# A three-stage transformer kernel on one Trainium2 core: first norm of the last stage made one stage earlier, turned context stored and reloaded, block rounding rewritten, order of the steps in the two last stages changed

## The reference

```python
x = x + tanh(g_xattn[0]) * mha16(layernorm(x), ctx)            # 16 heads of 32, with biases
x = x + tanh(g_ffn[0])   * ffn0(layernorm(x))                  # ternary weights, 8 bit activations, SiLU gate, 2048 wide
x = x + tanh(g_xattn[1]) * (softmax(layernorm(x) @ ctx.T) @ ctx)
x = x + tanh(g_ffn[1])   * (fp4(layernorm(x)) @ fp4(w1).T + bias)

def fp4(x):                                                    # blocks of 32 numbers
    amax  = max(abs(x), per block)
    scale = 2 ** (floor(log2(amax)) - 2) * 2 ** (0.5 * tanh(4 * delta))
    a     = clip(abs(x / scale), 0, 6)
    step  = 2 ** (clip(floor(log2(a)), 0, 2) - 1)
    return scale * sign(x) * round(a / step) * step
```

## Time and profile before

| | us |
|---|---|
| median of the runs | 1857.91 |
| profiled execution, its own time | 1863.25 |
| its span, first to last instruction | 1861.5 |
| last score starts to end of the span | 31.4 |

### The profile page before, as it was taken

The page is one execution under the profiler, slowest core; times in us unless marked ns, Lnnn a source line. Parts: engine busy times, 40 slices in busy tenths (PEclk is TensorE's granted clock), DMA queues, the critical chain, the costliest instruction groups (busy, mean ns, idle before and its releaser), DMA issues. The chain is left out here.

```text
span 1861.5 us, 27434 instructions
## 1 busy us (share of the span) xinstructions
PE 1575.9 (85%) x7400; PEld 1010.4 (54%) x7433; DVE 1330.4 (71%) x2277; ACT 868.4 (47%) x1433; POOL 898.3 (48%) x1098
## 2 busy tenths in 40 slices
PE   5889898989988899997257999999997588878886
PEld 3656555655655556652254544544443476666664
DVE  3676666757676667764755888888885488989886
ACT  3354545545554546544474545555453334444431
POOL 3265665656665666666002323223230366666653
PEclk9899998999999998997588999999998799999998
DMA  5627272543637272620802444444442212111110
GB/s 181 182 81 208 64 205 62 152 130 114 164 102 187 63 206 73 168 71 12 323 24 75 111 108 101 105 106 108 104 99 65 80 52 68 69 63 68 64 51 34
DMA packets 192668, 200.15 MB, mean 108 GB/s; under 512 B 94508, under 2 KB 111416, under 8 KB 192056
## 3 DMA queue, kind: packets, MB, share of 16 engines
q1 hardware_dynamic: 192568, 199.06, 38.4%
HBM read 119.05 MB, written 58.72 MB: 96 GB/s over the span
## 5 line engine op out<-in xcount | busy, mean ns | idle before, releaser
L488 ACT ACTIVATE a_probs<-a_sc 128x512 f32<-128x512 f32 x512 | 301.1, 596 | 330.5 <-PE a_sc L402 282.1
L543 DVE TENSOR_REDUCE a_negmax<-a_mx 128x1 f32<-128x512 f32 x512 | 337.5, 676 | 109.3 <-PE a_mx L385 107.3
L597 POOL TENSOR_TENSOR a_acc<-a_acc,a_probs 128x512 f32<-128x512 f32 x256 | 319.8, 1281 | 6.9 <-ACT a_probs L488 5.5
L597 POOL TENSOR_TENSOR a_acc<-a_probs 128x512 f32<-128x512 f32 x128 | 162.0, 1284 | 222.7 <-ACT a_probs L488 221.8
L385 PE MATMUL a_mx<-a_stack 96*128 96x512 f32 x512 | 230.2, 450 | 31.3 <-DVE a_negmax L543 19.5
L402 PE MATMUL a_sc<-a_stack 97*128 97x512 f32 x512 | 219.9, 432 | 29.5 <-DMA a_stack<-a_mrow 18.7
L962 PE MATMUL bank<-w_wgu,b_xq 128*128 128x512 bf16 x1022 | 230.7, 379 | 11.6 <-ACT b_sig L1001 10.5
L549 DVE RECIPROCAL a_attn<-a_den 128x128 f32<-128x128 f32 x128 | 120.8, 948 | 150.4 <-PE a_den L423 150.4
L962 PEld LDWEIGHTS bank<-w_wgu,b_xq 128*128 128x128 bf16 x1024 | 97.4, 98 | 139.9 <-ACT b_sig L1001 25.7
L385 PEld LDWEIGHTS a_mx<-a_stack 96*128 96x128 f32 x512 | 102.8, 201 | 103.7 <-DVE a_negmax L543 53.7
L1107 POOL TENSOR_TENSOR b_veps<-b_mv,w_eps 128x1 f32<-128x1 f32 x32 | 6.1, 190 | 298.6 <-DVE b_mv L1028 298.6
(11 more groups left out here) (175 smaller groups left out, 2974.7 us busy)
## 6 DMA issues: line engine op xcount, KB each, us to landing
a_stack<-spill SPq DMA_DIRECT2D x192, 256.0 KB, 4.9
spill<-a_part SPq DMA_DIRECT2D x64, 512.0 KB, 3.2
a_stage<-in_x_dram SPq DMA_DIRECT2D x32, 256.0 KB, 5.6
a_stage<-in_ctx_dram SPq DMA_DIRECT2D x32, 256.0 KB, 2.7
attn_t<-a_attn SPq DMA_DIRECT2D x32, 256.0 KB, 2.1
b_xin<-in_x_dram SPq DMA_DIRECT2D x32, 256.0 KB, 2.8
b_araw<-attn_t SPq DMA_DIRECT2D x32, 256.0 KB, 3.1
x_mid<-b_xo SPq DMA_DIRECT2D x32, 256.0 KB, 2.0
```

What stands on the lines that cost most here:

```text
L488: nc.scalar.activation(probs[:, k, j, :], sc[i % 2][:], ACT.Exp, scale=SCALE).then_inc(exp_done, 1)
L543: nc.vector.tensor_reduce(negmax[:, g % 2, j, t:t + 1], mx[i % 2][:], axis=AX.X, op=ALU.max, negate=True).then_inc(mx_done, 1)
L597: nc.gpsimd.tensor_tensor(acc[:, j], probs[:, 0, j] if k == 1 else acc[:, j], probs[:, k, j], ALU.add)\
```

## The change

Five edits:
1. The context, turned and split by `attention_phase`, is stored to DRAM as `ctx_t` in two pieces of 1 MB a batch (`ctstore`), and `final_phase` loads it as one transfer of 2 MB a batch (`ctload`). Its `cturn` step goes (PE, ACT, DVE); `csplit` keeps the copy of the context itself (ACT, POOL).
2. `ffn_phase` computes mean and reciprocal deviation of its own output (`ln2`: two DVE and four POOL instructions a tile) and stores two numbers a token once a batch (`nstore`, into `ln_mid`). `final_phase` loads them and does the first norm with one ACT instruction; the first `ln` goes from DVE and POOL.
3. In `ffn_phase` the bias of the norm moves from DVE to POOL (two small instructions more), the norm runs after the second Silu, and `split`, `quant`, `xcode` and `xturn` have new due times.
4. The rounding of `final_phase`: five DVE instructions become one ACT instruction (`mag`: absolute value times 2^22, written as bf16) and three DVE instructions.
5. New due times in `final_phase`. `yturn` runs a tile further back, `pv` and the block scales too, and the turned banks are three instead of four.

The order in steady state of `final_phase` after the change (tile distance in brackets):
- PE: `score`[0], `pv`[-1], `yturn`[-3], `xturn`[+1], `pturn`[0], `ffn`[-3].
- DVE: `quant` 0 [-3], output sum [-4], `quant` 1 and 2 [-3], block maximum [-2], row maximum [0], `scale` 1 to 3 [-2], reciprocal [0], sum after `pv`[-1], `ln`[-1], low parts of `xturn`[+1] and `pturn`[0].
- ACT: norm of `y`[-2], `csplit`[+3], norm of `xn`[+1], exponent [0], copies for `yturn`[-3], `xturn`[+1], `pturn`[0], `mag`[-2].
- POOL: product with block scale [-3], `csplit`[+3], inverse scale product and bias sum [-2], reciprocal times gate [0], `ln`[-1].

The order of `ffn_phase`: PE and SP as before. DVE: `down`[-2], `hcode`[-1], `ln2`[-2], `hid` 0, `hid` 1, `quant`[+1], `hid` 2, `hid` 3, `hmax`, `hquant`, `o`[+2], `ln1`[+2]. ACT: Silu 0, Silu 1, norm [+1], Silu 2, copy of `split`[+3], `quant`[+1], Silu 3, `xcode`[+1], `hquant`. POOL: `ln1`[+1], `ln2`[-2], `split`[+3].

```diff
@@ attention_phase @@
+        STORE_CT = (50, 57.5)
+        for n, slot_n in enumerate(STORE_CT):
+            ck.add(ahead(slot_n), 9, "ctstore", n)
+                    elif name == "ctstore":
+                        n, = args
+                        sync_wait(sp, held, t_lo, it, shift, 2 * T, 2 * T)
+                        sync_wait(sp, held, t_hi, it, shift, 2 * T, 2 * T)
+                        half = slice(n * C // 2, (n + 1) * C // 2)
+                        sp.dma_start(ctx_t[bass.ds(b, 1)].rearrange("o p (c n) -> (o p) c n", c=C)[:, half],
+                                     ct[:, half].rearrange("p c h s -> p c (h s)").bitcast(F32)).then_inc(ct_stored, 16)
@@ attention_phase, ACT, before the first context tile is written @@
+                            wait_count(act, ct_stored, it, shift, 2, 0, 16)
@@ ffn_phase @@
-        at = dict(load=-300, split=-205, o=-148, ln1=-107, norm=-88, quant=-79, xcode=-59, xturn=-51, gu=0, gu_step=13,
-                  hmax=64, hquant=82, hcode=107, hturn=118, down=173, store=210, x1=35, sig=14, hid=19,
-                  act_norm=2, act_quant=13, act_hquant=8, x2=31, pool_split=10, pool_ln=7)
+        at = dict(load=-300, split=-255, o=-148, ln1=-107, norm=-72, quant=-65, xcode=-45, xturn=-40, gu=0, gu_step=13,
+                  hmax=64, hquant=82, hcode=107, hturn=118, down=173, store=210, ln2=210, nstore=228, x1=35, sig=14, hid=19,
+                  act_norm=0, act_quant=13, act_hquant=8, x2=31, pool_split=10, pool_ln=7)
-                    elif name == "norm":
-                        wait_count(dve, ln_rstd, it, shift, T, t + 1)
-                        wait_count(dve, ln_done, it, shift, T, t)
-                        nc.vector.scalar_tensor_tensor(nbias[:], mv[:, 0:1], -1.0, rstd[:], ALU.mult, ALU.mult).then_inc(ln_bias, 1)
+                    elif name == "ln2":
+                        wait_count(dve, x2_done, it, shift, T, t + 1)
+                        wait_count(dve, n_mv, it, shift, T, t)
+                        nc.vector.bn_stats(stats2[:], xo[:, t % 2, :]).then_inc(n_stats, 1)
...
+                        nc.vector.bn_aggr(mv2[:], stats2[:]).then_inc(n_mv, 1)
+                        nc.gpsimd.tensor_tensor(nbias[:], nmean[:], rstd[:], ALU.mult).then_inc(ln_bias, 1)
+                    elif name == "ln2":
...
+                        nc.gpsimd.tensor_tensor(norm2[:, t, 0:1], veps2[:], mhalf[:], ALU.pow).then_inc(n_rstd, 1)
...
+                        nc.gpsimd.tensor_tensor(norm2[:, t, 1:2], nmean2[:], norm2[:, t, 0:1], ALU.mult).then_inc(n_done, 1)
@@ final_phase @@
-        at = dict(cload=-440, cload_step=99, cturn=-354, cturn_step=100, xload=-190, ln=-95, norm=-58, xturn=-44,
-                  score=0, recip=40, pturn=42, pv=62, ln2=104, norm2=118, scale=139, scale_step=4, quant=165,
-                  quant_step=11, yturn=251, ffn=337, store=351, max=26, exp=33, x3=26, out=18, act_turn=17,
-                  dve_turn=12, pool_scale=6, pool_quant=8, pool_ln=0)
+        at = dict(cload=-400, cload_step=99, csplit=-300, csplit_step=100, ctload=-420, xload=-190, norm=-70, xturn=-31,
+                  score=0, recip=58, pturn=74, pv=132, ln2=175, norm2=206, scale=(216, 236, 238, 240), mag=288, quant=(300, 305, 310),
+                  yturn=364, ffn=379, store=402, max=34, exp=44, x3=35, out=23, act_turn=6, act_split=20, pool_split=30,
+                  dve_turn=13, pool_scale=4, pool_quant=8, pool_ln=0)
+                    elif name == "ctload":
+                        h = t // T
+                        sync_wait(sp, held, s_full, it, shift, TT, t + T - TT)
+                        sp.dma_start(ct[:, h].rearrange("p c h s -> p (c h s)").bitcast(F32), ctx_t[bass.ds(b, 1)].rearrange("o p n -> (o p) n"))\
+                            .then_inc(ct_loaded[h], 16)
+                    elif name == "norm" and args[1] == 0:
...
+                        nc.scalar.activation(xn[:, t % R2, :], xr[:, t % XR, :], ACT.Identity, scale=norm1[:, h, k, 0:1],
+                                             bias=norm1[:, h, k, 1:2]).then_inc(xn_done, 1)
+                    elif name == "mag":
...
+                        nc.scalar.activation(mag[:, t % R2, :], y[:, t % R2, :], ACT.Abs, scale=MAGIC).then_inc(mag_done, 1)
@@ final_phase, DVE, quant @@
-                            nc.vector.tensor_scalar(u, u, FP4_MAX, -FP4_MAX, ALU.min, ALU.max).then_inc(quant_step, 1)
-                                nc.vector.tensor_scalar(m.bitcast(I32), u.bitcast(I32), EXP_BITS, None, ALU.bitwise_and).then_inc(quant_step, 1)
-                                nc.vector.tensor_scalar(m, m, 1.0, ROUND / 2, ALU.max, ALU.mult).then_inc(quant_step, 1)
-                                nc.vector.tensor_tensor(u, u, m, ALU.add).then_inc(quant_step, 1)
-                                nc.vector.tensor_tensor(u, u, m, ALU.subtract).then_inc(rounded, 1)
+                            nc.vector.scalar_tensor_tensor(u, m, 1.5 * MAGIC, u, ALU.max, ALU.subtract).then_inc(quant_step, 1)
+                            nc.vector.scalar_tensor_tensor(u, m, 1.5 * MAGIC, u, ALU.max, ALU.subtract).then_inc(quant_step, 1)
+                            nc.vector.tensor_scalar(u, u, FP4_MAX, -FP4_MAX, ALU.min, ALU.max).then_inc(rounded, 1)
```

More of the change, by code:

```diff
@@ L936, in window @@
                         sp.dma_start(x_out[bass.ds(b, 1), t * P:(t + 1) * P, :], xo[:, t % 2, :]).then_inc(stored[t % 2], 16)
+                    elif name == "nstore":
+                        sync_wait(sp, held, n_done, it, shift, T, T)
+                        sync_wait(sp, held, n_rstd, it, shift, T, T)
+                        with nc.allow_non_contiguous_dma(reason="two numbers a token, once a batch"):
+                            sp.dma_start(ln_out[bass.ds(b, 1)].rearrange("o p n -> (o p) n"), norm2[:].rearrange("p t n -> p (t n)"))\
+                                .then_inc(n_stored, 16)
                 ck.run(sp, window)
+                sp.wait_ge(n_stored, NB * 16)
                 for s in stored:
@@ L1431, in window @@
                                                        ALU.mult, ALU.add).then_inc(out_done, 1)
-                ck.run(dve, window, dict(score=at["max"], pv=at["x3"], ffn=at["out"], xturn=at["dve_turn"], pturn=at["dve_turn"], cturn=at["dve_turn"]))
+                ck.run(dve, window, dict(score=at["max"], pv=at["x3"], ffn=at["out"], xturn=at["dve_turn"], pturn=at["dve_turn"]))
             @block.gpsimd
```

220 lines of the change are left out of this document (124 added, 96 removed).

## The result

| | before | after |
|---|---|---|
| median of the runs, us | 1861.61 (1854.94 to 1865.76) | 1735.82 (1735.12 to 1737.90) |
| span of the profiled execution, us | 1861.5 | 1733.3 |
| ratio to before | | 0.9326, 95% interval 0.9299 to 0.9353 |

The change takes 126 us, 6.7%. The prediction said 77. It had the sign and the main mechanism, and its range ended at 1765.

The account below looks back on a forecast made before the run. DVE was taken to bound the last stage, PE the first feed-forward. -73.2 (last stage) - 7.4 (first feed-forward) + 2.5 + 0 + 1 (ends) = -77.1 us from 1863.25, 1786.2; against the median 1857.91, 1781 us; range 1765 to 1812.

Parts of the forecast that it names:

- the exponent is out in time: Last stage: exponent out at 4.5 us of the step, PE asks at 6.7, so its 1.65 us of waiting go.
- (a): Last stage: POOL holds both new rounding instructions, DVE has 10.0 us a tile; 29.5 us more, 1810; chance 0.17.
- (b): First feed-forward: a loop of DVE and ACT sets the step, 13.9 us; 1808, likelier 1795; chance 0.10.
- (d): Attention: stores of the turned context delay `mrow` on SP's queue and stop PE; +107 us, 1888; chance 0.03.
- the size of PE's step: Last stage: PE's 9.70 us a tile less 0.45 for one group of transposes, 9.25; bounds 9.04 and 9.70.
- the loop's ends: Last stage: 6 us added for three back edges of the hardware loop; bounds 0 and 9.
- attention at 0: Attention: the two pieces of 1 MB stored a batch cost 0; bounds 0 and 107 us.
- the five waits: First feed-forward: PE's idle 1.47 us before a gate product at five loop starts goes; -7.4 us.
- Rival (c): Last stage: a loop of handoffs, not DVE's load, sets the step, which stays near 11.5 us; 1854; chance 0.05.
- my layout of one step: Last stage: one step of 9.25 us laid out in the new order; no handoff holds it, least slack 1.0 us.
- Ends: Around the last stage's start: waiting for `nstore` +2.5 us; first load to first score 17.6 us, so 0.
- the +1: End of the last stage: gains `mag` and a wait for the bias sum, loses two rounding steps; bounds -2 and +4.

Follow-up runs that it names:

- more_pe: The kernel after with the four transposes of `yturn` made twice a tile in the last stage, more work for PE; 1750.11 us, ratio 0.9400.
- more_dve: The kernel after with one more full-width DVE reduction a tile in the last stage, its output unused; 1733.01 us, ratio 0.9309.
- after_old_round: The kernel after with the five old rounding instructions on DVE in place of the three new ones; 1744.42 us, ratio 0.9377.
- att_only: The kernel before with only the attention of after: two stores a batch and ACT's wait for them; 1842.91 us, ratio 0.9924.
- round_only: The kernel before with only the new rounding of the last stage, in the old order; 1831.17 us, ratio 0.9855.
- after_old_both: The kernel after with the old due times of the last stage and the five old rounding instructions; 1822.35 us, ratio 0.9790.
- after_old_order: The kernel after with the old due times of the last stage, the new rounding kept; 1793.31 us, ratio 0.9645.

## Why the prediction was right and wrong

- *Right:* PE takes over the last stage and nothing else is late; the exponent is out in time. Shown by more_pe and more_dve. Of the rivals, (a) is false (0.68 each, not 1.3 or more). The hold falls on the narrow scale steps instead, so DVE is busy 90.99 x 8.73 / 100 = 7.94 us a tile and not 7.3, which costs nothing. The Trainium skill, "SBUF — State Buffer", section "Who interferes with whom", says that DVE and GpSimd share one pair of ports, which the first to issue keeps for its whole instruction. The traces agree for the narrow scale steps, and for clip and mask, 1.02 and 0.82 in before against 0.42 and 0.43 in after_old_round. (b) is false: the first feed-forward takes 13.17 us a tile, not 13.9, and PE is busy 200 of 200 us. (d) is false: att_only loses nothing.
- *Wrong, the size of PE's step:* "It is busy 84.21 / 8.68 = 9.70 us a tile", less 0.45. Busy time contains modelled ends before each wait and each change of bank. The distances between starts, in rows of before that I had and didn't use, give the step:

```profile
1608.85 0.60 PE L1245 MATMUL bank<-w_ident,c_craw 128*128 128x128 f32 x4
1609.28 0.60 PE L1245 MATMUL bank<-w_ident,c_y 128*128 128x128 f32 x4
...
1613.31 2.92 PE L1272 MATMUL bank<-c_ct,c_xt 128*128 128x512 f32 x12
1616.07 2.04 PE L1292 MATMUL bank<-w_w,c_yt 128*128 128x512 f32 x8
```

  12 products are 1616.07 - 1613.31 = 2.76, a turn 0.43, the feed-forward's 8 products 8/12 of 2.76, 1.84: 2 x 2.76 + 3 x 0.43 + 1.84 = 8.65. It measured 8.73. The term was mis-sized by 0.52 x 31 = 16 us.
- *Wrong, the loop's ends:* +6 for three of them. They and all else beyond 31 steps of 8.73 cost 0.3 us (steps of 8.81, and of 9.04 and then 8.44), since the slack takes them: 5.7 less. The first three steps of the stage run at 5.8 to 8.3, 3.8 us less. Together with the step this is the 25.6 us by which the stage was missed. The prediction also put the 9 us by which the steps of before exceed 31 x 11.52 at the ends of loop and stage; a part of them are the eight steps with the clock at 0.86.
- *Wrong, attention at 0:* 20 us. The waits were in the trace of before; I had looked at what the edit adds there and not at what ACT already waited for.
- *Wrong, the first feed-forward:* the five waits were sized right at 7.4. The term left out 0.15 us in every step, in which the gate products took 6.87 us from their start to the next `o` and take 6.72 after, and the start of the stage: 6.4 us. That the 0.15 was Silu coming late is likely; no wait is recorded there.
- *Right for a wrong reason:* "So the last stage goes by DVE, 11.52 us a tile". The reading that DVE's load alone sets the step fell (round_only, after_old_both). Rival (c), a ring of handoffs, had hold of the mechanism and the wrong result: such a ring does hold the old order at 10.6 when the load is gone, and the new order, edit 5, opens it. The forecast of PE's step needed only that the new order has no such ring, and my layout of one step checked that.
- *Ends:* `nstore` left 2.35 us behind the last store for the 2.5 expected, and from the first load to the first score were 17.35 us for 17.6; the 2 MB landed in 7.9 for 8.5. The last tile's chain is 2.7 us longer than the +1 allowed.

## What to carry to other kernels

Take the step of an engine that will become the bound from the distances between starts in rows without a wait, never from its busy share. A high busy share of an in-order engine doesn't prove that its load is the bound: here 3.3 us a tile less on DVE moved the step by 0.9 us until the order changed, so follow one full turn of the waits, across queue neighbours as well as data. And before you price an edit at nothing, read what the engines it touches already wait for, "issue" included.

## What the hardware showed

- ACT stood still for 10.4 to 10.9 us at the start of four loop iterations. The instruction queue fetched 18 pieces of some 8 KB from 280 to 660 us, and in the pause read the DMA engines were 90% or more busy; a shift by four instructions ended it, worth 1% of the time. The Trainium skill, "Runtime: NRT & Kernel Launch", section "Instruction fetch mechanics", says that a taken branch to a target outside the two pages held makes the engine wait for a fetch. The pauses at a loop's start agree with that; that 4, 32 and 128 instructions all end them isn't told by it.
- A DVE instruction on 16 numbers a row took 1.25 us beside a POOL instruction of 1.29, and 0.17 in after_old_order where POOL was idle.
- The back edge of the hardware loop cost 0.1 us with PE full (8.81 for 8.73), and up to 2.7 in the kernel before.
- In the kernel before, steps of the last stage with a mean granted clock of 0.86 took some 0.5 us more than those at 1.00.
